# A new order table for the first loop of a fused two-layer kernel, with the setup's loads, memory sets and semaphore priming put in other places

## The chip, the cores and the metric

The kernel runs on one core of one Trainium2 chip, as one launch. The metric is the device time of that launch in microseconds (us), as a median of several runs. Lower is better.

## The reference

Sixteen images of 224x224 are cut into 196 patches each and projected to 192 channels, and 128 text tokens are put behind them: 324 tokens of 192 channels for each of 16 batches. Four residual blocks follow, each behind a layer norm.

```python
h = tok(x, W); h = concatenate([h, txt], axis=1)
h = h + L0_attn(layernorm(h))    # softmax over tokens, circular convolution with V (done by DFT), projection
h = h + L0_ffn(layernorm(h))     # 192 -> 768, gelu, -> 192
h = h + L1_attn(layernorm(h))    # 12 heads of 16; keys and values also of 196 shared tokens; softmax
h = h + L1_ffn(layernorm(h))     # 4 experts take half of the tokens each by router probability (top_k);
                                 # MLP 768 and a second attention on what they took, combined by the gate
```

## The kernel before, in words

The program has two software-pipelined loops over the 16 batches. The first does everything up to the router probabilities and the attention with shared tokens; the second does the experts' layer. In the turn between them (two iterations) both loops' work is woven together by position in their tables. TensorE (PE), ScalarE (ACT), VectorE (DVE), GpSimd (POOL) and SyncE (SP, which only issues DMAs) each run the same list of words, `ORDER_1` for the first loop, and each engine does in list order what it has to do for a word. The order among engines is set by semaphores alone.

`ORDER_1` has 15 slots. The words:

- `s`: one of 60 score products of a batch (PE, one matmul into one of two `sps` banks, L1356), then an exponential on ACT (L944). The third `s` waits for the exponential of the first.
- `a`: four attention sums of the four scores of the slot before (PE, L1371, eight half passes). Where a group of heads ends, ACT copies them to `av`.
- `m`: a product of queries and keys for the row maxima (PE, L1390, into one of three `mps` banks), reduced by DVE (L1214). Slots 0 to 4 do the heads of group 1, slots 5 to 9 those of group 2, slots 10 to 14 those of group 0 of the next batch. After the 18th of a group DVE does five small steps (L1220 to L1228); `r` transposes the result on PE, and ACT copies and stores it into `qpack` by a DMA. The scores of that group need it.
- `p`: one step of the expert choice on DVE, in six late iterations only.
- the rest are steps of the layers, each for the batch that `OFF_1` gives (this one, the one before, or one or two ahead): `tok`, `ln1`, `t1`, `zv`, `val`, `zs`, `zt`, `dft`, `of`, `inv`, `proj` make the first block two batches ahead; `ln2`, `t2`, `hid`, `out` the second, `ln3`, `t3`, `qk`, `todram`, `pack0`, `pack1` the queries and keys of the next batch, `v` and `pack2` those of this one; `den`, `recip`, `spread`, `norm`, `proj4`, `ln4`, `hx`, `t4`, `t5`, `log`, `exp`, `prob`, `prt` finish the batch before.

Steps write into two `lin` banks in turn, so each waits until the step two before it has been copied out.

The way from `qk` to the next maxima leaves the engines: ACT rounds a part to bf16 (`piece`, L854), DVE takes the rest (L1045), POOL splits that twice (L767, L769), SP stores the pieces (`scr_q` L596, `scr_k` L600) and, when they have landed, loads them as `qpack` and `kpack` for group 0 (L611, L614). Only then can the first `m` of slots 10 to 14 run.

The first iteration (number -2) does only the first block of batch 0, and number -1 adds the second and the queries of batch 0; full iterations are numbers 0 to 14.

Before the loop, SP primes 81 semaphores one after the other (L560, L561) and then issues all weight loads (L562 on): seven of them, `FIRST`, count on one semaphore, and PE waits for all seven before its first matmul, which is `tok`. DVE sets eight tensors to zero, and POOL loads the first batch and sets 13 tensors (L729 to L738), among them `kpack` twice, with `minus_half` last; `reciprocal_roots` (L771) needs `minus_half`.

Of the kernel before, what the change touches and what calls it, by code (L numbers as in the profile page):

```python
# [10 lines left out]
KC = 96  # L11
KP = 128
H, D = 12, 16
NK1 = N + SC
TK1, KT1 = P, 5
LAST1 = NK1 - (KT1 - 1) * TK1
# [17 lines left out]


ORDER_1 = (
# [15 lines left out]
)  # L52
OFF_1 = {"den": -1, "recip": -1, "spread": -1, "norm": -1, "proj4": -1, "ln4": -1, "hx": -1, "t4": -1, "t5": -1,
         "log": -1, "exp": -1, "prob": -1, "prt": -1, "v": 0, "pack2": 0, "hab": 0,
# [31 lines left out]
def number(name):  # L86

    tail = name[len(name.rstrip("0123456789")):]
    return int(tail) if tail else 0
# [172 lines left out]
def build(nc, A):  # L262
# [3 lines left out]
    with ctx:  # L266
# [3 lines left out]
        primed = []  # L270

        def signal(name, per=1, prime=1, first=0):
            s = Signal(ctx.enter_context(nc.semaphore(name)), per, prime - first, first)
            if per and prime:
                primed.append(s)
            return s


        w_tok = sb("w_tok", [128, 2, C])
        w_a = sb("w_a", [KP, 2, H])  # L280
        w_v0 = sb("w_v0", [KP, 2, C])
# [13 lines left out]
        ident = sb("ident", [128, 128])  # L295
        identb = sb("identb", [128, 128], bf16)
        dft = sb("dft", [KP, T, 2, 2, FW])
# [5 lines left out]
        bc = sb("bc", [128, GROUPS, N])  # L303
# [14 lines left out]
        xS = sb("xS", [KP, 2, NK1])  # L318
# [179 lines left out]
        def comes_first(att, j):  # L498

            return att is two and isinstance(j, int) and j == 0  # L500

        loads_first, loads, setup_dve, setup_pe, setup_act, setup_pool, sc_first, sc_rest, sc_mid, sc_pieces, sc_scr, sc_pack = (
            signal(n, 0) for n in ("loads_first", "loads", "setup_dve", "setup_pe", "setup_act", "setup_pool", "sc_first",
                                   "sc_rest", "sc_mid", "sc_pieces", "sc_scr", "sc_pack"))
        x_in = signal("x_in", 48, prime=0)
        hab_ready = signal("hab_ready", 16)
# [33 lines left out]
        MEMSETS_POOL, SETUP_POOL, SETUP_DVE = 13, 17, 9  # L540
        block = ctx.enter_context(nc.Block())

        FIRST = [(w_tok, A["w_tok"]), (ident, A["ident"]), (w_a, A["w_a"]), (w_v0, A["w_v0"]), (dft, A["dft"]),
                 (idft, A["idft"]), (w_p0, A["w_p0"])]
        LOADS = [
            (w_in, A["w_in"]), (b_in, A["b_in"]), (w_qkv, A["w_qkv"]), (w_out, A["w_out"]),
# [10 lines left out]

        @block.sync
        def _(sp):
            for s in primed:  # L560
                sp.sem_inc(s.sem, s.at(s.first, 0) + s.passed)  # L561
            for dst, src in FIRST:  # L562
                sp.dma_start(dst.ap(), src).then_inc(loads_first.sem, 16)
            for dst, src in LOADS[:4]:
# [158 lines left out]
        def _(pool):  # L723
# [3 lines left out]
                pool.dma_start(hin[:, 2, :], A["txt"][j, 2 * P - IMG:TXT, :]).then_inc(x_in.sem, 16)  # L727

            load_x(0)  # L729
            for n, (x, value) in enumerate(((of[64:KP, :, :, :], 0.0), (aT[KC:KP, :, :], 0.0), (aT[KC:KC + 1, :, :], 1.0),  # L730
                                            (xS[KC:KP, :, :], 0.0), (v1[:, :, :, :], 0.0),
                                            (kpack[KC:KP, :, :], 0.0), (yA[KC:KP, :, :], 0.0),
                                            (v1[:, 0:KT1 - 1, :, D:D + 1], 1.0), (v1[0:LAST1, KT1 - 1, :, D:D + 1], 1.0),
                                            (kpack[6 * D:6 * D + 3, :, :], 1.0), (yA[KC:KC + 1, :, :], 1.0),
                                            (bc[:, :, :], 1.0), (minus_half[:, :, :], -0.5))):
                if n:
                    pool.wait_ge(setup_pool.sem, n)
                nc.gpsimd.memset(x, value).then_inc(setup_pool.sem, 1)  # L738
            pool.wait_ge(setup_pool.sem, MEMSETS_POOL)

            def shared_pieces():

# [42 lines left out]
            def first_step(name, k, c, what, j, i):  # L785
                if name == "shared":
                    shared_pieces()
                    both_layers()
                elif name in ("ln1", "ln2", "ln3", "ln4"):
                    if k == 1:  # L790
                        reciprocal_roots(number(name) - 1, j)
                elif name == "xload":

                    front.filled(pool, i, "tok")
                    pool.wait_ge(ln1_done.sem, ln1_done.at(j - 1, 1))
                    front.emptied(pool, i, "proj_1")
                    pool.sem_inc(gate_pool.sem)
                    load_x(j)
                elif name == "hx":
                    pool.wait_ge(ln4_done.sem, ln4_done.at(j, 1))  # L800
                    pool.wait_ge(spilled.sem, spilled.at(j, 0))
                    nc.gpsimd.tensor_tensor(hx[:, :, :], ha[:, :, :], xna[:, :, :], ALU.add).then_inc(hx_ready.sem, 1)
                elif name == "qk":
                    parts(one, front, j, i, k)
# [18 lines left out]

        @block.scalar
        def _(act):
            def shared_keys():

                for m, p in enumerate(SCK):
                    act.wait_ge(setup_pe.sem, m + 1)
                    nc.scalar.copy(piece[0:p, m, 0, 0:SC], mps[0:p, m, 0:SC]).then_inc(sc_first.sem, 1)  # L830
                act.wait_ge(setup_pool.sem, MEMSETS_POOL)
                for m, p in enumerate((TK1, LAST1)):
                    act.wait_ge(setup_pe.sem, m + 3)
                    nc.scalar.copy(v1[0:p, KT1 - 2 + m, :, 0:D],
                                   sps[0:p, m, 0:C].rearrange("p (h d) -> p h d", d=D)).then_inc(setup_act.sem, 1)
# [141 lines left out]
        def _(dve):  # L977
# [5 lines left out]

            def shared_keys():

                dve.wait_ge(loads_first.sem, 16 * NFIRST)
                nc.vector.tensor_copy(identb[:, :], ident[:, :]).then_inc(setup_dve.sem, 1)
                for m, p in enumerate(SCK):
                    dve.wait_ge(sc_first.sem, m + 1)
                    nc.vector.tensor_tensor(rest[0:p, m, 0:SC], mps[0:p, m, 0:SC], piece[0:p, m, 0, 0:SC],  # L990
                                            ALU.subtract).then_inc(sc_rest.sem, 1)
# [287 lines left out]
        @block.tensor  # L1279
        def _(pe):  # L1280
            mm = nc.tensor.matmul
            pe.wait_ge(loads_first.sem, 16 * NFIRST)
            pe.wait_ge(setup_dve.sem, SETUP_DVE - 1)
            pe.wait_ge(setup_pool.sem, 3)

# [121 lines left out]
            def first_step(name, k, c, what, j, i):  # L1407
# [14 lines left out]
                elif name == "t1":  # L1422
                    pe.wait_ge(ln1_done.sem, ln1_done.at(j, 1))
                    transposes(front, i, what, k, xn1)
                elif name == "zv":
                    front.emptied(pe, i, "t1_1")
                    b = front.bank(pe, i, what)
                    for f in range(2):
# [200 lines left out]
```

## Time and profile before

| | us |
|---|---|
| median of 3 runs | 2089.15 (2087.38 to 2093.47) |
| the profiled execution, own time | 2096.61 |
| its span, first to last instruction | 2094.9 |
| PE busy | 1871.9 (89%) |
| DVE / ACT / POOL busy | 1247.5 / 1110.8 / 289.3 |

The span is what the trace covers; about 1.7 us of the execution's own time lie around it. The busy time of PE contains modelled ends of pipelined matmuls, so it overstates the work. In a view, a number in square brackets is the idle time of the engine just before the line's first instruction, and behind the arrow stands what ended it. Times of the trace count from the start of the span.

### The profile page before, as it was taken

The numbers are of one execution on the slowest core, as the hardware profiler recorded it, in microseconds if no ns is written. First come the engines' busy times: TensorE is split into PE (matmuls) and PEld (weight loads), VectorE is DVE, ScalarE is ACT, GpSimd is POOL, SyncE is SP. The second block draws the span as 40 slices with busy tenths as digits, with TensorE's granted clock in tenths as the row PEclk, the third lists the DMA queues.
The fourth block names the chain that finished last, engine by engine and source line by source line (L and its number), as shares of the span: only waits on it lengthen the run. The fifth ranks groups of instructions, "written<-read, shape, count | busy, mean of one in ns | idle before, by whom it ended". The sixth has DMA issues, their size and how long they took to land. (4 is left out here: it accounts for less than half of the span.)

```text
span 2094.9 us, 41506 instructions
## 1 busy us (share of the span) xinstructions
PE 1871.9 (89%) x11904; PEld 1260.5 (60%) x11904; DVE 1247.5 (60%) x3509; ACT 1110.8 (53%) x2583; POOL 289.3 (14%) x441
## 2 busy tenths in 40 slices
PE   3788998998998998998998997868999999999996
PEld 2565665675665675665675664435666666666664
DVE  2256566666566566666676674535767666666563
ACT  1244555555554555555555554445556565666663
POOL 4201111111111111111111110100100011001000
PEclk9799999999999999999999998879999999999998
DMA  4202212212212212212212202202433334333331
GB/s 151 68 16 58 69 32 71 64 32 74 61 32 67 64 36 69 67 34 69 65 36 69 68 27 76 75 17 80 103 100 90 87 93 119 82 101 101 100 86 36
DMA packets 161303, 143.61 MB, mean 69 GB/s; under 512 B 32284, under 2 KB 136488, under 8 KB 161064
## 3 DMA queue, kind: packets, MB, share of 16 engines
q1 hardware_dynamic: 157448, 136.69, 24.1%
q0 software_dynamic: 2304, 4.79, 1.0%
q8 instruction: 58, 0.95, 0.2%
q10 hardware_dynamic: 1440, 0.75, 0.1%
q14 instruction: 53, 0.43, 0.1%
HBM read 82.79 MB, written 50.16 MB: 63 GB/s over the span
## 5 line engine op out<-in xcount | busy, mean ns | idle before, releaser
L944 ACT ACTIVATE prob<-sps 108x324 f32<-108x324 f32 x1536 | 621.3, 439 | 506.6 <-PE sps L1356 470.3
L1214 DVE TENSOR_REDUCE mxh<-mps 108x1 f32<-108x324 f32 x1152 | 519.7, 489 | 319.2 <-PE mps L1390 315.4
L1356 PE MATMUL sps<-qpack,kpack 128*108 128x324 bf16 x1536 | 436.3, 318 | 33.5 <-ACT prob L944 25.6
L1390 PE MATMUL mps<-kpack,qpack 96*108 96x324 bf16 x1728 | 391.1, 296 | 46.7 <-DMA kpack<-scr_k 28.9
L1356 PEld LDWEIGHTS sps<-qpack,kpack 128*108 128x108 bf16 x1536 | 189.7, 127 | 228.2 <-ACT prob L944 163.0
L1371 PE MATMUL aps<-prob,v 128*32 128x324 f32 x3072 | 320.0, 460 | 2.4 <-DVE gmall L1202 1.1
L1390 PEld LDWEIGHTS mps<-kpack,qpack 96*108 96x108 bf16 x1728 | 215.8, 131 | 175.8 <-issue 57.6
L1342 PE MATMUL lin<-yT,w 128*128 128x324 f32 x576 | 184.0, 450 | 18.3 <-ACT g L844 14.1
L1214 DVE TENSOR_REDUCE mxs<-mps 108x2 f32<-108x392 f32 x288 | 160.0, 555 | 53.9 <-PE mps L1390 53.7
L1342 PEld LDWEIGHTS lin<-yT,w 128*128 128x128 f32 x576 | 102.4, 192 | 64.4 <-issue 33.2
L767 POOL CAST piece<-rest 128x324 bf16<-128x324 f32 x96 | 43.7, 456 | 700.2 <-DVE rest L1045 695.9
L1371 PEld LDWEIGHTS aps<-prob,v 128*32 128x32 f32 x3072 | 72.6, 109 | 104.5 <-issue 57.7
L1342 PE MATMUL lin<-xT,w_in 128*128 128x324 f32 x384 | 121.6, 449 | 0.5 <-ACT xT L840 0.5
L1332 PE MATMUL lin<-w,g 128*108 128x192 f32 x576 | 107.9, 328 | 0.7 <-PEq L136 0.7
L1332 PE MATMUL lin<-w_out,g 128*108 128x192 f32 x576 | 105.9, 327 | 1.6 <-PEq L136 1.6
L1332 PEld LDWEIGHTS lin<-w_out,g 128*108 128x108 f32 x576 | 92.3, 174 | 3.3 <-issue 2.1
L1332 PEld LDWEIGHTS lin<-w,g 128*108 128x108 f32 x576 | 91.2, 173 | 3.5 <-issue 1.1
L958 ACT COPY av<-aps 128x324 f32<-128x324 f32 x96 | 41.2, 429 | 98.0 <-PE aps L1371 73.0
L776 POOL TENSOR_SCALAR vars<-mean 108x3 f32<-108x3 f32 x64 | 15.5, 242 | 561.6 <-DVE mean L1012 560.9
L944 ACT ACT_TABLE_LOAD x64 | 82.1, 1283 | 14.9 <-PE sps L1356 13.1
L1315 PE MATMUL lin<-ident,xn 108*96 108x108 f32 x384 | 56.2, 263 | 36.9 <-DVE xn L1017 25.9
L1342 PEld LDWEIGHTS lin<-xT,w_in 128*128 128x128 f32 x384 | 69.8, 194 | 29.7 <-ACT g L844 6.4
(150 smaller groups left out, 2354.8 us busy)
## 6 DMA issues: line engine op xcount, KB each, us to landing
qpack<-scr_q SPq DMA_DIRECT2D x96, 243.0 KB, 3.2
kpack<-scr_k SPq DMA_DIRECT2D x96, 121.5 KB, 3.3
scr_q<-piece SPq DMA_DIRECT2D x32, 243.0 KB, 2.9
scr_k<-piece SPq DMA_DIRECT2D x32, 243.0 KB, 3.5
kpack<-scr_k SPq DMA_DIRECT2D x96, 81.0 KB, 3.1
bc<-rec_d SPq DMA_DIRECT2D x112, 60.8 KB, 2.4
scr_q<-piece SPq DMA_DIRECT2D x32, 162.0 KB, 3.3
scr_q<-piece SPq DMA_DIRECT2D x64, 81.0 KB, 3.0
```

The costliest lines, as they stand in the source:

```text
L767: nc.gpsimd.tensor_copy(piece[:, m, 1, :], rest[:, m, :]).then_inc(att.second.sem, 1)
L776: nc.gpsimd.tensor_scalar(vars4[:, n, 0], mean[n][:, :, 1], EPS4, None, ALU.add).then_inc(vars_known[n].sem, 1)
L944: nc.scalar.activation(prob[0:rows, n % NP, :], sps[0:rows, n % 2, 0:N], ACT.Exp, scale=SCALE).then_inc(att.exped.sem, 1)
L958: nc.scalar.copy(av[:, q, :], aps[:, 0:N]).then_inc(att.copied.sem, 1)
L1214: nc.vector.tensor_reduce(dst, src, AX.X, ALU.max, negate=True).then_inc(att.mps.free["dve"].sem, 1)
L1315: done = nc.tensor.transpose(b[0:KC, t * P:(t + 1) * P], src[:, t, k * KC:(k + 1) * KC], ident[0:P, 0:P])
L1332: done = mm(tiles2(b)[0:P, t % 2, :], acts[k][:, t * P:(t + 1) * P], weights[k], start=k == 0, stop=k == 5)
L1342: done = mm(b[0:size, 0:N], w[:, k, c:c + size], x[:, k, 0:N], start=k == 0, stop=k == 1)
L1356: mm(sps[0:rows, n % 2, 0:N], kpack[:, 4 * q + n % 4, k * att.rows:k * att.rows + rows], qpack[:, 4 * q + n % 4, :], start=True, stop=True ...
L1371: mm(aps[32 * hd:32 * hd + 32, 0:N], att.values[:, k, 4 * q + hd, :], prob[:, n % NP, :], start=k == 0, stop=k == kt - 1).then_inc(att.sum ...
L1390: done = mm(bank[0:P, s * SC:s * SC + k1 - k0], qpack[0:6 * D, 4 * q + hd, t * P:(t + 1) * P], kpack[0:6 * D, 4 * q + hd, k0:k1], start=Tr ...
```

## The change

The words of `ORDER_1` are the same, in another order and in other slots. In the setup, SP no longer primes the semaphores: ACT does it, at its own beginning. The seven first loads are split into two (`TOKENS`: `w_tok` and `ident`) and five (`FIRST`), on semaphores of their own; PE waits at the beginning for the two, and for the five at the first `zv`. POOL's memory sets are split: four (`of`, twice `aT`, `minus_half`) at once, and nine behind the reciprocal root of batch 0's first norm.

```diff
 ORDER_1 = (
-    "a ln2_1 m m m s v_0.0 s ln2_3 s s v_0.1 m s m p v_1.0 s recip s",
-    "t2_0 m a s t2_1 m m s",
-    "m s a s hid0 m hid1 pack2",
-    "m hid2 shared hid3 s m s hid4 m m p norm a m",
-    "hid5 m s s m proj4_0.0 m den proj4_0.1 s spread0 spread1 proj4_1 s s ln4_0 a s ln4_1 r ln4_2 hx s",
-    "out_0.0 m m out_0.1 a m p out_0.2 ln4_3 out_0.3 m out_1.0 m out_1.1",
-    "s m s ln3_0 tok.0 s tok.1 m m s hab t4_0 t4_1 ln3_1 s m a m log m s t5_0",
-    "exp p m s s ln3_3 t5_1 s m s a",
-    "s prob m t3_0 hc m s t3_1 a ln1_0 m qk0 m m qk1 s s qk2 s s ln1_1 p r",
-    "s todram s prt a s s",
-    "a s t1_0 t1_1 s s ln1_3 zv s",
-    "val_0.0 zs val_0.1 s val_1 pack0 zt s m m m dft_0.0 m p pack1 m a m s m dft_0.1 m s m dft_1.0 m m",
-    "m dft_1.1 s of s a s",
-    "s m s m m a s inv_0.0 s m p s m s m s",
-    "inv_0.1 inv_1.0 inv_1.1 s r proj_0.0 proj_0.1 proj_1 xload s ln2_0 a",
+    "den ln2_1 m m m spread0 a s s v_0.0",
+    "m s m s m p s v_0.1 s ln2_3 recip m m v_1.0 s s t2_0 a pack2 s",
+    "s a m s t2_1 s m m m s shared hid0 hid1",
+    "m m hid2 p hid3 hid4 hid5 norm m s m a s",
+    "m spread1 proj4_0.0 proj4_0.1 m proj4_1 s out_0.0 ln4_0 s out_0.1 out_0.2 ln4_1 s out_0.3 ln4_2 a s s r",
+    "m out_1.0 p m m m out_1.1 ln4_3 m a t4_0 ln3_0 t4_1 m s m s tok.0",
+    "ln3_1 m s tok.1 m m s t5_0 ln3_3 hab m s a",
+    "hc t5_1 log p s exp m m t3_0 t3_1 m prob hx s s m m qk0 m ln1_0 s qk1 s qk2 m s s a s ln1_1 todram s prt s s s p",
+    "r a s",
+    "a s s t1_0 t1_1 ln1_3",
+    "a",
+    "s zv s val_0.0 val_0.1 zs s val_1 m s m s zt m m m s dft_0.0 m p s m dft_0.1 m m s m dft_1.0 m m m s dft_1.1 m a",
+    "of pack0 s s a m s s m",
+    "m s a s inv_0.0 m p s",
+    "s pack1 inv_0.1 s inv_1.0 inv_1.1 r a s proj_0.0 xload proj_0.1 proj_1 ln2_0 s",
 )
...
-        FIRST = [(w_tok, A["w_tok"]), (ident, A["ident"]), (w_a, A["w_a"]), (w_v0, A["w_v0"]), (dft, A["dft"]),
+        TOKENS = [(w_tok, A["w_tok"]), (ident, A["ident"])]
+        FIRST = [(w_a, A["w_a"]), (w_v0, A["w_v0"]), (dft, A["dft"]),
                  (idft, A["idft"]), (w_p0, A["w_p0"])]
...
         def _(sp):
-            for s in primed:
-                sp.sem_inc(s.sem, s.at(s.first, 0) + s.passed)
+            for dst, src in TOKENS:
+                sp.dma_start(dst.ap(), src).then_inc(loads_tok.sem, 16)
             for dst, src in FIRST:
                 sp.dma_start(dst.ap(), src).then_inc(loads_first.sem, 16)
...
+            FEW = ((of[64:KP, :, :, :], 0.0), (aT[KC:KP, :, :], 0.0), (aT[KC:KC + 1, :, :], 1.0), (minus_half[:, :, :], -0.5))
+            REST = ((xS[KC:KP, :, :], 0.0), (v1[:, :, :, :], 0.0), (kpack[KC:KP, :, :], 0.0), (yA[KC:KP, :, :], 0.0),
+                    (v1[:, 0:KT1 - 1, :, D:D + 1], 1.0), (v1[0:LAST1, KT1 - 1, :, D:D + 1], 1.0),
+                    (kpack[6 * D:6 * D + 3, :, :], 1.0), (yA[KC:KC + 1, :, :], 1.0), (bc[:, :, :], 1.0))
...
+            memsets(FEW, 0)
...
                     if k == 1:
                         reciprocal_roots(number(name) - 1, j)
+                        if name == "ln1" and isinstance(i, int) and i == -2:
+                            pool.wait_ge(root_known[0].sem, root_known[0].at(j, 1))
+                            memsets(REST, len(FEW))
...
         def _(act):
+            for s in primed:
+                act.sem_inc(s.sem, s.at(s.first, 0) + s.passed)
...
-            pe.wait_ge(loads_first.sem, 16 * NFIRST)
+            pe.wait_ge(loads_tok.sem, 16 * len(TOKENS))
             pe.wait_ge(setup_dve.sem, SETUP_DVE - 1)
             pe.wait_ge(setup_pool.sem, 3)
...
                 elif name == "zv":
+                    if isinstance(i, int) and i == -2:
+                        pe.wait_ge(loads_first.sem, 16 * NFIRST)
```

## Rows read from the trace of the kernel before

**Rows 1.** The page, its first line.

```profile
span 2094.9 us, 41506 instructions
```

**Rows 2.** Windows: stretch, length, busy us of PE, PEld, DVE, ACT, POOL; clock; DMA; GB/s.

```profile
121.60:1276.00 1154.40, 1060.59 (x7093) 729.09 (x7091) 736.93 (x2148) 631.64 (x1512) 174.05 (x276) 0.99 0.20 55
1276.00:1416.00 140.00, 105.26 (x505) 56.84 (x506) 61.71 (x162) 55.98 (x124) 12.63 (x18) 0.76 0.21 54
```

**Rows 3.** Windows of one full iteration, cut behind `qk2` and at the first group-0 `m`.

```profile
434.90:480.70 45.80, 45.03 (x311) 32.26 (x304) 30.80 (x93) 27.87 (x64) 8.11 (x13) 1.00 0.16 49
480.70:494.40 13.70, 9.81 (x62) 5.25 (x60) 4.83 (x18) 7.90 (x22) 3.90 (x7) 1.00 0.52 144
494.40:513.00 18.60, 17.14 (x121) 12.34 (x125) 14.23 (x35) 7.01 (x19) 0.00 (x0) 1.00 0.04 9
```

**Rows 4.** Timeline of the start: start us, duration, engine, line, operation.

```profile
6.14 1.99 SPq L563 DMA_DIRECT2D w_tok<-in_w_tok  x1
...
6.54 0.33 DVE L981 MEMSET work<- 64x330 f32 x1
...
8.31 5.30 POOL L738 MEMSET kpack<- 32x6240 bf16 x1
...
10.54 0.43 SPq L563 DMA_DIRECT2D w_p<-in_w_p  x1
...
15.68 2.90 PE L1418 MATMUL lin<-w_tok,pT 128*108 128x192 f32 x8 [15.68 <-DMA w_p<-in_w_p]
...
20.79 0.31 DVE L1012 BATCH_NORM_AGGREGATE mean<-st 108x2 f32<-108x6 f32 x3 [0.73 <-DVEq L140]
...
21.79 0.11 POOL L738 MEMSET minus_half<- 108x6 f32 x1
22.21 0.25 POOL L776 TENSOR_SCALAR vars<-mean 108x3 f32<-108x3 f32 x1 [0.31 <-POOL minus_half L738]
```

**Rows 5.** DMA issues of the first 100 us, last column us from issue to landing.

```profile
w_tok<-in_w_tok SPq DMA_DIRECT2D x1, 192.0 KB, 4.0
w_p<-in_w_p SPq DMA_DIRECT2D x1, 192.0 KB, 5.1
```

**Rows 6.** Timeline of the way from `qk` to the next maxima, ACT, POOL, DVE, SP.

```profile
479.77 0.43 ACT L854 CAST piece<-lin 128x324 bf16<-128x324 f32 x1 [0.92 <-PE lin L1342]
...
480.26 0.80 POOL L769 TENSOR_TENSOR piece<-rest,piece 128x324 bf16<-128x324 f32 x1
...
480.38 0.71 DVE L1220 TENSOR_TENSOR mx<-mxh,mxs 108x12 f32<-108x12 f32 x1
...
481.09 4.94 SPq L596 DMA_DIRECT2D scr_q<-piece  x6
...
482.01 0.90 DVE L1045 TENSOR_TENSOR rest<-lin,piece 128x324 f32<-128x324 f32 x2
...
484.51 0.80 POOL L769 TENSOR_TENSOR piece<-rest,piece 128x324 bf16<-128x324 f32 x1
...
486.08 1.24 SPq L600 DMA_DIRECT2D scr_k<-piece  x2
```

**Rows 7.** Timeline of PE in the same iteration.

```profile
439.95 0.44 PE L1356 MATMUL sps<-qpack,kpack 128*108 128x324 bf16 x2
...
440.77 0.75 PE L1371 MATMUL aps<-prob,v 128*32 128x324 f32 x8
441.45 0.34 PE L1356 MATMUL sps<-qpack,kpack 128*108 128x324 bf16 x1
...
494.31 0.65 PE L1390 MATMUL mps<-kpack,qpack 96*108 96x324 bf16 x4 [1.16 <-DMA kpack<-scr_k]
```

**Rows 8.** Timeline of PE at `inv` and `proj`.

```profile
505.58 0.79 PE L1454 MATMUL lin<-idft,of 128*96 128x162 f32 x4 [0.55 <-DVE of L1132]
...
510.47 2.20 PE L1323 MATMUL lin<-w_p,aT 128*108 128x192 f32 x12 [0.74 <-DVE aT L1138]
```

**Rows 9.** Timeline of DVE at `recip`.

```profile
440.82 0.38 DVE L1054 RECIPROCAL drec<-dsm 108x36 f32<-108x36 f32 x1 [0.31 <-DMA dsm<-av]
```

More of the change, by code:

```diff
@@ L500, in comes_first @@
             return att is two and isinstance(j, int) and j == 0
-        loads_first, loads, setup_dve, setup_pe, setup_act, setup_pool, sc_first, sc_rest, sc_mid, sc_pieces, sc_scr, sc_pack = (
-            signal(n, 0) for n in ("loads_first", "loads", "setup_dve", "setup_pe", "setup_act", "setup_pool", "sc_first",
+        loads_tok, loads_first, loads, setup_dve, setup_pe, setup_act, setup_pool, sc_first, sc_rest, sc_mid, sc_pieces, sc_scr, sc_pack = (
+            signal(n, 0) for n in ("loads_tok", "loads_first", "loads", "setup_dve", "setup_pe", "setup_act", "setup_pool", "sc_first",
                                    "sc_rest", "sc_mid", "sc_pieces", "sc_scr", "sc_pack"))
@@ L729, in _, with memsets @@
             load_x(0)
[L730 to L739, printed above, removed]
+            FEW = ((of[64:KP, :, :, :], 0.0), (aT[KC:KP, :, :], 0.0), (aT[KC:KC + 1, :, :], 1.0), (minus_half[:, :, :], -0.5))
+            REST = ((xS[KC:KP, :, :], 0.0), (v1[:, :, :, :], 0.0), (kpack[KC:KP, :, :], 0.0), (yA[KC:KP, :, :], 0.0),
+                    (v1[:, 0:KT1 - 1, :, D:D + 1], 1.0), (v1[0:LAST1, KT1 - 1, :, D:D + 1], 1.0),
+                    (kpack[6 * D:6 * D + 3, :, :], 1.0), (yA[KC:KC + 1, :, :], 1.0), (bc[:, :, :], 1.0))
+            def memsets(sets, done):
+                for n, (x, value) in enumerate(sets):
+                    if n + done:
+                        pool.wait_ge(setup_pool.sem, n + done)
+                    nc.gpsimd.memset(x, value).then_inc(setup_pool.sem, 1)
+                pool.wait_ge(setup_pool.sem, done + len(sets))
+            memsets(FEW, 0)
+            assert len(FEW) + len(REST) == MEMSETS_POOL
             def shared_pieces():
@@ L984, in shared_keys @@
             def shared_keys():
-                dve.wait_ge(loads_first.sem, 16 * NFIRST)
+                dve.wait_ge(loads_tok.sem, 16 * len(TOKENS))
                 nc.vector.tensor_copy(identb[:, :], ident[:, :]).then_inc(setup_dve.sem, 1)
```

## The prediction, on record before the changed kernel ran

> **What bounds the kernel now.** I read the windows first. The eleven hundred microseconds of the first loop's full iterations have PE busy 1060.6 of 1154.4 us, DVE 736.9, ACT 631.6 [rows 2]: PE is the engine nearest to its limit. One full iteration, cut in three, lasts 45.8 + 13.7 + 18.6 = 78.1 us [rows 3], and 15 of them (numbers 0 to 14) carry the loop. The reader should see that the middle piece is different: PE is busy 9.8 of 13.7 us there, idle 3.9 us, while it is idle only 0.8 us in the 45.8 before it and 1.5 us in the 18.6 after it. The timeline of that piece shows why: the chain ACT `piece`, DVE `rest`, POOL's splits, SP's stores and loads [rows 6], at whose end PE's first group-0 `m` at 494.31 is released by the DMA of `kpack` [rows 7]. What PE has to do meanwhile is hidden; whatever shortens the chain, or fills it with work taken from elsewhere, shortens the iteration. The second such place is `inv` and `proj`, released by DVE's `of` and `aT` [rows 8]. The start has PE waiting until 15.68 for `w_p`, the last of seven loads [rows 4].
>
> **The start.** SP's first load is issued at 6.14, behind the priming [rows 4]. With the priming on ACT it can go at about 0.9, where the priming began (81 steps in 5.25 us). All loads move up by 5.2. `w_tok` landed 4.0 us after issue [rows 5], so it lands near 5, and `ident`, issued 2 us later, near the same time. PE still waits for DVE's eight sets, the last of which ends at 6.54 + 0.33 = 6.87 [rows 4]. ACT's priming ends near 6.1, before its first copy is due. So PE starts at 6.9 instead of 15.7: -8.7 us. The five other loads ended with `w_p` at 10.54 + 5.1 = 15.6 [rows 4, 5], now 10.4; `zv` wanted them 10.9 us after the first matmul, now at about 17, so that wait costs nothing. Second, the variance of the first norm was ready at 20.79 + 0.31 = 21.10, but POOL began its root at 22.21, behind `minus_half` [rows 4]. POOL is free now; elsewhere this step follows the variance by 0.2 us, so -0.9. The chain from the first `tok` to the end of iteration -2 is one of single steps with nothing beside it, so all of it goes through: -9.6 us in sum.
> The nine sets moved behind the root keep POOL for 16.2 us (from 5.53 to 21.73 before), so from about 13 to 30. What is queued behind them on POOL is `xload` of the next batch, which was due at 49.2 and is now due at 39.6: cover of 9 us. PE wants the sets at the end of iteration -2, later still. If that cover were gone, each us of it would cost one.
> A row bears on what else the sets may do. DVE's step L1220, which reads two tensors, took 0.71 us and ended at 481.09, beside a POOL instruction that ran from 480.26 to 481.06 [rows 6]; four sister steps behind it take 0.17 each. One engine held the other up. In iteration -2, DVE now works beside memory sets of up to 5.30 us [rows 4], which no row shows. If one such set held up DVE's norm or its `zexp` scaling, the cost would be 0 to 5.3 us. I take 0, for DVE's sets ran at 0.33 us beside POOL's before, and keep 5.3 for the range.
> The Trainium skill, page "SBUF — State Buffer", section "Who interferes with whom", says that DVE and GpSimd share one pair of SBUF ports as an exclusive lock: a GpSimd instruction that only writes does not disturb a DVE instruction with two SBUF inputs, but does block one in a two-port mode. By the first half the sets cost nothing, by the second a copy or scaling of DVE could wait a whole set, the 5.3 us above; the row at L1220 agrees with the lock.
>
> **The middle piece.** Before, the 18th `m` of group 2 stands before `qk1` in the table, so DVE does the closing steps (L1220 on) before it takes the `rest` of `qk1`: that began at 482.01, though ACT's piece was ready at 479.77 + 0.43 = 480.20 [rows 6]. 1.8 us lost. POOL's three pairs then end at 485.31, SP's stores at 487.32. In the new table the 18th `m` stands behind `qk2`, and `ln1_0` (0.87 us) stands between `qk0` and `qk1`. Step by step, counted from the end of `qk0`: DVE had the `rest` of `qk1` at +4.1; now it has its piece at +2.1, behind a reduction and `ln1_0` at about +3.0. POOL's second pair ends near +4.85 instead of +6.15. There SP takes over as the limit: six stores took 4.94 us and two more 1.24 [rows 6], and the first three are not earlier than before. I take 1.0 us gained, 0 and 1.8 as the bounds.
> Second, work moved into the piece. Before: 12 `s`, 2 `a`, `r`, `prt`, two `t1`, `zv`, three `val`, `zt` between `qk2` and the first group-0 `m`. Now: 13 `s`, 4 `a`, one `m`, and no `zt`. Before `qk2`, one `m` and a few `s` go the other way. An `s` takes 0.14 us of PE (the second in 0.44 less 0.30), an `a` 441.45 - 440.77 = 0.68 [rows 7]. So +0.14 + 2 x 0.68 + 0.15 - 0.25 = +1.4, and with `m` and `s` around `qk1` (one `m` less) about +1.2 net from the end of `qk0`. It fits: PE's idle time there was 3.9. Sum for the piece: -2.2 us an iteration. The `r` of group 2 is now further back, but `s` of group 1's end and two `a` follow it, 3.0 us of work before the first `s` of group 2 needs the DMA of `mT`; before it was 2.2 us of work. No new cost.
>
> **`of` to `proj`.** `dft_1.1` to `inv_0.0` had 2.7 us of PE work between; now 3.6. From the start of `inv_0.0` to `proj_0.0` passed 510.47 - 505.58 = 4.9 us [rows 8] with 3.7 of work; DVE was working off six `m` and the closing steps before it reached `aT`. Now four `m` stand behind `of`, and an `a` and an `s` stand between `inv_1.1` and `proj_0.0`: 3.9 of work, ready after about 4.2. That is -0.5 and -1.0: -1.5 us.
>
> **What crowds.** I counted, from the two tables, the places where PE meets an `m` with less than 1.65 us of its work since the one three before (three reductions of DVE of about 0.5): four before, nine now, short by 0.8 and 2.3 us in sum. For `s` with less than 0.9 us since the one two before: seven before (2.0 us), five now (1.5). Net +1.0. `log` now has only 0.8 us of work between it and `t3_1`, which needs its bank, and `proj4_0` to `out_0.0` 1.2 instead of 2.6: +0.3. Together +1.3 us, bounds 0 and 2.6.
> `den` and `spread0` now stand before `pack2` in SP's queue, so `pack2` waits for `recip`, some 7 us later than before; the `m` of group 2 want it 24 us into the iteration, so this is covered. The `recip` stands two `m` later on DVE, which waited 0.31 us for `dsm` [rows 9]; `den` is issued behind three `m` more, 0.4 us later. Nothing is taken for it.
>
> **The sum.** An iteration: -2.2 - 1.5 + 1.3 = -2.4 us; 15 of them -36. The start -9.6. In the turn (140 us, PE busy 105 [rows 2]) both tables' words are interleaved by position, and there is no `qk` of the first loop in it: 0, with 5 either way. The second loop's table is unchanged: 0. Together -46 us. The profiled execution has a span of 2094.9 [rows 1] in 2096.6, 7.5 above the median; I take the difference against the median: 2089 - 46 = 2043 us.
>
> **Rivals.**
> Only the start pays: the new table takes with its crowding what it gives (-3.7 + 3.7). For it speaks that the limit in an order of this kind moves quickly from one short place to the next, against it that the chain through DMA is seen as one long idle stretch. 2089 - 9.6 = 2079, with 2070 to 2082 for an iteration within 0.6 us.
> The crowding costs nothing: -3.7 x 15 - 9.6 = -65, 2024. For it: DVE is busy only 64% of the loop.
> The first sets hold up DVE at the start: up to 5.3 back, 2048. Its place is within the forecast's range; chance 0.1 of its own, by the page's second half. So far the trace bears out only the lock between two readers.
> Slower: `recip` at its new place stops DVE in front of the `m`. PE can run three `m` ahead and then stands, so each us that `dsm` comes later than DVE's turn costs one. Before, it came 0.31 us late [rows 9]. It decides from (36 + 9.6) / 15 = 3.0 us late in each iteration, and over 0.3% slower from 3.5: 2089 + 7 = 2096 and more. Against it: 0.4 to 0.9 us is what I count.
> The edit of the start doing nothing (PE held by the sets of DVE alone, which end at 6.87) can be excluded down to 8 us by the rows; I leave it in the ranges.
>
> **How the numbers follow.** Forecast, 2030 to 2060: 0.5. Between it and the start alone, 2060 to 2070: 0.1. Only the start: 0.17. No crowding, under 2030: 0.1. Slower by a stop that I have misjudged, `recip` the named one: 0.1, and 0.03 for no change. The change must exceed 0.3% (6 us), about what a measurement of this kernel can tell from none. Faster 0.86, same 0.04, slower 0.10. Range 2022 to 2080, which leaves out the slower cases and a little at the lower end.
>
> **What would show it.** PE's first matmul at 6.9 and POOL's first root 0.2 us behind the variance. The nine sets beside DVE's steps of iteration -2 with unchanged durations. A period near 75.7 us in place of 78.1; `rest` of `qk1` within 1 us of its piece; PE's idle time before the first group-0 `m` down to 2.5 us or less; the idle before `proj` gone. Wrong would be: DVE idle before `recip` for more than 1 us, more idle time of PE at `m` behind `mxh` in slots 1 to 3 and 5, or a turn longer than 145 us.

## The result, and the profile after

The changed kernel takes 2019.8 us (median of 4 runs, 2012.9 to 2025.5), the kernel before beside it 2091.3 (4 runs, 2087.4 to 2096.6): a ratio of 0.9655, 95% interval 0.9617 to 0.9693, so 71.5 us less. Forecast were 46 us less, 2043, with a range of 2022 to 2080. The sign was right; the size was not, and the time lies just below the range. One of the four runs of `n_max_crowded` below took 6039 us and is left out of its numbers; no other run of any kernel stood apart like this.

The page of the changed kernel, its first part (the profiled execution took 2019.94 us):

```profile
span 2018.3 us, 41467 instructions
...
PE 1844.5 (91%) x11904; PEld 1249.0 (62%) x11904; DVE 1257.5 (62%) x3509; ACT 1080.0 (54%) x2555; POOL 288.9 (14%) x441
```

The two profiled spans differ by 76.6 us [rows 1], 5 more than the medians, since the profiled execution of the kernel before was a long one. To see where, I took an instruction that occurs once for each batch, ACT's exponential `zexp` (in the first block of batches 0 to 15). Its row of the changed kernel, with the first and the last start, and then that of the kernel before:

```profile
L912 ACT ACTIVATE zexp<-lin,nmz x16: 521/521/522, 28.1 to 1134.4; 12x324 f32<-12x324 f32 x16
```

```profile
L900 ACT ACTIVATE zexp<-lin,nmz x16: 522/522/522, 29.5 to 1199.4; 12x324 f32<-12x324 f32 x16
```

With the starts between them, the first `gelu` of the second loop's batch 1 as the end of the turn, and the start of DVE's last step as the end of the last stretch (3.8 us before the end of the span in both), the time splits like this. The last two columns are the time at the lower clock, 1.2 GHz, inside each stretch (us):

| stretch | before | after | less | forecast | at 1.2 GHz before | after |
|---|---|---|---|---|---|---|
| start, to `zexp` of batch 0 | 29.5 | 28.1 | 1.4 | 9.6 | 0 | 12.9 |
| to batch 1 | 69.0 | 64.3 | 4.7 | 0 | 27.4 | 16.5 |
| to batch 2 | 77.6 | 67.9 | 9.7 | 2.4 | 13.6 | 4.8 |
| to batch 15, 13 periods | 1023.3 | 974.3 | 49.1 | 31.2 | 13.7 | 34.1 |
| rest of the loop and the turn | 167.4 | 159.8 | 7.6 | 2.4 | 41.0 | 30.7 |
| to the end | 724.2 | 720.2 | 4.0 | 0 | 47.8 | 41.0 |

The last line is no effect of the change: its stretch came out between 719.6 and 728.0 us in the kernels below that have the new table, and between 719.5 and 724.2 in those that have the old one. The reader should see two errors of opposite sign: the start gave 8 us less than forecast, the loop much more.

One full iteration of the changed kernel, cut as in [rows 3], the next iteration whole, and the stretches that answer to [rows 2]:

```profile
408.25:451.20 42.95, 42.25 (x282) 30.90 (x281) 30.43 (x92) 24.09 (x58) 7.84 (x13) 1.00 0.19 52
451.20:464.30 13.10, 11.22 (x79) 5.66 (x78) 5.89 (x19) 8.29 (x23) 4.17 (x7) 1.00 0.54 152
464.30:481.92 17.62, 17.44 (x130) 12.58 (x129) 13.75 (x35) 8.33 (x21) 0.00 (x0) 1.00 0.04 8
481.92:558.97 77.05, 73.74 (x490) 51.38 (x488) 50.08 (x145) 40.82 (x101) 12.00 (x19) 0.96 0.20 57
1200.00:1342.00 142.00, 103.45 (x555) 55.26 (x552) 62.66 (x170) 64.89 (x144) 12.05 (x19) 0.83 0.23 60
115.00:1210.00 1095.00, 1046.34 (x7081) 723.71 (x7081) 739.34 (x2141) 596.90 (x1477) 173.12 (x275) 0.98 0.21 59
```

At full clock an iteration is 42.95 + 13.10 + 17.62 = 73.7 us, not 75.7 as forecast and 78.1 before. PE is idle 0.7, 1.9 and 0.2 us in the three pieces (0.8, 3.9 and 1.5 before). The second iteration has the same instructions and takes 3.4 us more; its clock is 0.96, and a cut in steps of 10 us shows why (two rows of it):

```profile
510.00:520.00 10.00, 9.62 (x82) 7.40 (x80) 9.12 (x27) 4.96 (x13) 2.49 (x3) 1.00 0.14 49
520.00:530.00 10.00, 9.40 (x44) 5.84 (x44) 7.87 (x26) 5.99 (x17) 3.70 (x6) 0.83 0.27 84
```

The clock drops to 1.2 GHz for part of 520 to 530, and again in 540 to 550, while PE was busy 9.62 of the 10 us before the first of them and 8.04 of the 10 before the second. Such stretches add up to 34 us between 150 and 1130 us, 14 before. That is why the mean of the 13 periods is 74.9 and not 73.7.

PE's waits between 300 and 1100 us (what it waited for: us in sum, times, longest), first before, then after:

```profile
PE mps L1390 <- DMA kpack<-scr_k: 15.1, 10, 1.9
PE sps L1356 <- ACT prob L944: 12.5, 30, 0.6
PE lin L1315 <- DVE xn L1017: 10.9, 10, 1.1
PE lin L1323 <- DVE aT L1138: 6.9, 10, 0.7
PE lin L1454 <- DVE of L1132: 5.3, 10, 0.6
```

```profile
PE mps L1402 <- DMA kpack<-scr_k: 14.7, 11, 2.6
PE lin L1327 <- DVE lg L1187: 5.1, 10, 0.6
PE sps L1368 <- ACT prob L956: 3.5, 18, 0.2
PE mps L1412 <- DVE mp L1240: 2.7, 7, 0.4
PE mps L1402 <- DVE mxh L1226: 1.0, 6, 0.2
```

Here lies the largest surprise: the wait at the end of the chain through DMA, on which I had built the forecast, is hardly smaller. Those for `of` and `aT`, nearly all of that for the norm's `xn`, and most of that of the scores for ACT's exponentials are gone. A new one, `lg`, stands behind `log` (I had priced its bank, together with that of `out_0.0`, with 0.3 us of crowding): 0.5 us an iteration.

The start of the changed kernel, to be read beside [rows 4]:

```profile
0.88 0.42 SPq L562 DMA_DIRECT2D w_tok<-in_w_tok  x1
...
6.54 0.33 DVE L993 MEMSET work<- 64x330 f32 x1
...
8.46 2.86 PE L1430 MATMUL lin<-w_tok,pT 128*108 128x192 f32 x8 [8.46 <-DMA hin<-in_txt]
...
13.20 0.31 DVE L1024 BATCH_NORM_AGGREGATE mean<-st 108x2 f32<-108x6 f32 x3 [0.40 <-DVEq L140]
...
13.79 0.25 POOL L782 TENSOR_SCALAR vars<-mean 108x3 f32<-108x3 f32 x1 [8.16 <-DVE mean L1024]
14.12 0.90 POOL L788 TENSOR_TENSOR root<-vars,minus_half 108x3 f32<-108x3 f32 x1
15.05 8.21 DVE L1029 TENSOR_SCALAR xn<-hin,mean,root 108x192 f32<-108x192 f32 x3 [1.54 <-POOL root L788]
15.07 0.96 POOL L741 MEMSET xS<- 32x1040 f32 x1
16.09 1.70 POOL L741 MEMSET v<- 128x1920 f32 x1
17.85 5.29 POOL L741 MEMSET kpack<- 32x6240 bf16 x1
...
24.31 5.29 POOL L741 MEMSET kpack<- 3x6240 bf16 x1
...
28.89 0.89 DVE L1122 TENSOR_SCALAR zexp<-zexp,zrec 12x324 f32<-12x324 f32 x1
```

POOL's root follows the variance (13.20 + 0.31) by 0.28 us, as forecast. PE begins at 8.46, not 6.9: it waits for the first batch, which POOL loads. And DVE's three scalings `xn`, begun at 15.05, end at 23.26, 0.12 us behind the set of `kpack` that ended at 23.14. Taken singly they last 1.10, 1.83 and 5.43 us, beside sets of 0.96, 1.70 and 5.29, and each ends 0.11 to 0.12 us behind its own set. The third:

```profile
17.82 5.43 DVE L1029 TENSOR_SCALAR xn<-hin,mean,root 108x192 f32<-108x192 f32 x1
```

Likewise the scaling of `zexp` ends at 29.78, behind the next set of `kpack` (29.60). The kernel with the old setup does the first in 0.96 and the second in 0.38 us (next section).

### The profile page after: what moved, and what is told of

It is laid out like the page before. It is cut to its first block and busy times, and to the rows that moved or that the text cites. A ratio compares the mean times of both kernels' runs of the same rounds, so it can differ in the third digit from the quotient of the medians.

```text
span 2018.3 us, 41467 instructions
## 1 busy us (share of the span) xinstructions
PE 1844.5 (91%) x11904; PEld 1249.0 (62%) x11904; DVE 1257.5 (62%) x3509; ACT 1080.0 (54%) x2555; POOL 288.9 (14%) x441
## 5 line engine op out<-in xcount | busy, mean ns | idle before, releaser
L1402 PE MATMUL mps<-kpack,qpack 96*108 96x324 bf16 x1728 | 385.2, 297 | 47.2 <-DMA kpack<-scr_k 24.6
L1368 PEld LDWEIGHTS sps<-qpack,kpack 128*108 128x108 bf16 x1536 | 184.8, 127 | 213.3 <-ACT prob L956 118.0
L1383 PE MATMUL aps<-prob,v 128*32 128x324 f32 x3072 | 298.9, 454 | 3.9 <-DVEq L140 1.1
L1354 PE MATMUL lin<-yT,w 128*128 128x324 f32 x576 | 183.7, 450 | 13.5 <-ACT g L856 11.5
L1383 PEld LDWEIGHTS aps<-prob,v 128*32 128x32 f32 x3072 | 66.4, 108 | 85.9 <-issue 62.5
L1354 PE MATMUL lin<-xT,w_in 128*128 128x324 f32 x384 | 111.8, 441 | 0.2 <-ACT g L856 0.2
L1460 PE MATMUL lin<-vz,dft 128*82 128x204 f32 x384 | 83.3, 358 | 0.7 <-DVEq L140 0.7
```

Source lines behind the costliest of these rows:

```text
L1354: done = mm(b[0:size, 0:N], w[:, k, c:c + size], x[:, k, 0:N], start=k == 0, stop=k == 1)
L1368: mm(sps[0:rows, n % 2, 0:N], kpack[:, 4 * q + n % 4, k * att.rows:k * att.rows + rows], qpack[:, 4 * q + n % 4, :], start=True, stop=True ...
L1383: mm(aps[32 * hd:32 * hd + 32, 0:N], att.values[:, k, 4 * q + hd, :], prob[:, n % NP, :], start=k == 0, stop=k == kt - 1).then_inc(att.sum ...
L1402: done = mm(bank[0:P, s * SC:s * SC + k1 - k0], qpack[0:6 * D, 4 * q + hd, t * P:(t + 1) * P], kpack[0:6 * D, 4 * q + hd, k0:k1], start=Tr ...
L1460: done = mm(b[0:FW, 256 * c:256 * c + C + H], dft[:, t, k, c, :], vz[:, t, :], start=t == 0, stop=t == T - 1)
```

## The experiments

Ratios are to the kernel before, timed in the same session, with 95% intervals. "Iteration" is the undisturbed one, at full clock, the median of a trace, from `zexp` to `zexp`. The changed kernel has three such iterations among its 13 (73.2 to 73.6 us). The four traces of kernels that share its table have medians of 73.6 to 74.0 (`table_only` 73.8, `sets_after_zs` 73.9, `sets_first` 74.0), so a difference to 73.6 that is given below may be up to 0.4 us too large.

### The parts alone: setup_only and table_only

`setup_only` has the old table with the new setup, `table_only` the new table with the old setup.

> The new setup with the old order table. Theory: in the changed kernel POOL's nine memory sets hold up DVE's first norm (8.2 us for three steps that took 0.96), so the new setup brings little: the first exponential of zexp 1.4 us earlier, 0 to 3 us in all, 2088 to 2091. Rival: the setup also shortens the following iterations (priming, loads out of the way), 5 to 15 us.

> The new order table with the old setup. Theory: the table carries nearly all of the gain, -68 to -72 us, 2020 to 2023. Rival: the two parts need each other, and the table alone gives 50 to 60 us.

Measured: 2090.0 us, 0.9995 (0.9976 to 1.0014), and 2023.0 us, 0.9680 (0.9648 to 0.9712). In `setup_only` `zexp` of batch 0 starts at 28.65, 0.9 us earlier than before. The whole gain lies in the table, the two together add up within their error, and my 9.6 us for the start are not there. From `setup_only` and from `table_only`, the same step of DVE:

```profile
15.64 8.21 DVE L1029 TENSOR_SCALAR xn<-hin,mean,root 108x192 f32<-108x192 f32 x3 [1.53 <-POOL root L788]
```

```profile
23.47 0.96 DVE L1017 TENSOR_SCALAR xn<-hin,mean,root 108x192 f32<-108x192 f32 x3 [3.41 <-POOL root L782]
```

The table also shortens the turn by itself (158.9 us of the stretch that had 167.4), and so it does the second interval (69.4 for 77.6).

### Where the sets stand: sets_after_zs and sets_first

```diff
 # sets_after_zs: POOL's nine sets behind zexp's scaling of batch 0
-    pool.wait_ge(root_known[0].sem, root_known[0].at(j, 1))
+    pool.wait_ge(zs_ready.sem, zs_ready.at(j, 1))
     memsets(REST, len(FEW))
 # sets_first: all nine directly behind the four
     memsets(FEW, 0)
+    memsets(REST, len(FEW))
 # and behind the root
-    pool.wait_ge(root_known[0].sem, root_known[0].at(j, 1))
-    memsets(REST, len(FEW))
```

> The changed kernel with the nine memory sets behind the scaling of zexp of batch 0 instead of behind the first root. Theory (a set of POOL blocks DVE's tensor_scalar steps): the first norm takes 0.96 us again, zexp scaling 0.38, and everything behind it is 7 to 8 us earlier, 2012. Theory's further sign: of, whose steps read two tensors, now lies beside the sets and keeps 0.55 us a step, since the sets read nothing. Rival (any DVE step with a tensor in SBUF is blocked): of takes up to 5 us longer and the gain is 2 to 3 us.

> The changed kernel with all 13 memory sets at the beginning, minus_half fourth. Theory: POOL's root waits for the sets until about 21.8, as before the change, the norm follows undisturbed at 23.1, zexp about where it is in the changed kernel plus 1 us: 0 to +2 us, 2021. Rival: the sets cost DVE's own memory sets and the token copy more than that, +5 us.

Measured: 2015.9 us, 0.9651 (0.9615 to 0.9688), and 2024.1 us, 0.9668 (0.9630 to 0.9705). From `sets_after_zs`:

```profile
14.61 0.96 DVE L1029 TENSOR_SCALAR xn<-hin,mean,root 108x192 f32<-108x192 f32 x3 [1.53 <-POOL root L788]
20.75 0.52 ACT L912 ACTIVATE zexp<-lin,nmz 12x324 f32<-12x324 f32 x1 [2.91 <-DVE nmz L1117]
21.59 0.38 DVE L1122 TENSOR_SCALAR zexp<-zexp,zrec 12x324 f32<-12x324 f32 x1
22.02 0.96 POOL L741 MEMSET xS<- 32x1040 f32 x1 [7.45 <-DVE zexp L1122]
24.80 5.29 POOL L741 MEMSET kpack<- 32x6240 bf16 x1
29.18 0.55 DVE L1133 TENSOR_TENSOR ta<-vf 82x384 f32<-82x384 f32 x1
```

`zexp` starts at 20.75 instead of 28.06: with no set beside them the scalings take 0.96 and 0.38 us again, and the 7.3 us come back. `ta`, a step of DVE with two inputs, takes 0.55 us though the set of `kpack` runs from 24.80 to 30.09. So the cause is the set beside a scaling, not a set beside any step of DVE. The Trainium skill, page "SBUF — State Buffer", section "Who interferes with whom", says just this: a GpSimd instruction that only writes holds up no two-input step of DVE but blocks one in a two-port mode for its whole length; the trace agrees, with 8.21 for 0.96 us on one side and 0.55 us unchanged on the other, but no row says in which mode a scaling ran. Nor do the rows show the scaling as the later of the two: each of the three begins 0.02 us before its set (15.05 and 15.07, 16.07 and 16.09, 17.82 and 17.85), and it is the scaling that waits. In `sets_first` the norm stands behind all sets, undisturbed, and begins at 23.53, where it began before the change. In the medians these 7 us are small: 2015.9 against 2019.8, with intervals that overlap; the place of the sets is shown by the trace, its worth in the time only roughly.

### The middle piece: n_max_before_qk1, n_sums_out, n_norm_behind_qk2

All three edit slot 7 of the new table: the 18th `m` of group 2 back before `qk1`; one `a` moved out, before `qk0`; the norm behind `qk2`.

```diff
-m m qk0 m   ln1_0 s qk1 s qk2 m s s a s
+m m qk0 m m ln1_0 s qk1 s qk2   s s a s          (n_max_before_qk1)
+m m a qk0 m ln1_0 s qk1 s qk2 m s s s            (n_sums_out)
+m m qk0 m s qk1 s qk2 ln1_0 m s s a s            (n_norm_behind_qk2)
```

> The changed kernel with one word of slot 7 moved back: the 18th m of group 2 before qk1 and not behind qk2, as in the old table. Theory (the chain of DMAs sets the first group-0 m, and DVE's closing steps in front of the rest of qk1 lengthen it): the time from the end of qk0 to that m goes from 15.8 to 16.5 us or more, an iteration becomes 0.7 to 1.0 us longer, 10 to 15 us in all, 2031 to 2035. Rival (SP's stores are the limit, DVE's place has no part in it): under 0.2 us an iteration, within 3 us.

> The changed kernel with one a (0.68 us of PE) moved from behind qk2 to before qk0, out of the stretch that the DMAs set. Theory (PE waits there for the DMA whatever it does meanwhile): +0.7 us an iteration, +10 us, 2030. Rival (that stretch is set by PE and ACT, not by the DMA): no change within 3 us.

> The changed kernel with ln1_0 behind qk2 and not between qk0 and qk1. Theory (DVE's place in the chain sets the loads): the rest of qk1 begins at +2.6 us from the last pass of qk0, not +3.4; POOL is free from +3.5, so the pieces end 0.6 us earlier; -0.3 to -0.6 us an iteration, -5 to -9 us. Rival (SP's stores, which take 3.3 us behind the first three, or t1's norm, now later, become the limit): within 3 us, or slower.

Measured: `n_max_before_qk1` 2050.9 us, 0.9821 (0.9788 to 0.9854), an iteration 2.0 us longer on average, twice what I had expected. All of it lies between the start of `qk0` and the first group-0 `m`: 18.8 us (median) in place of 16.7. Counted from the third of the four passes of `qk0` (here and below), DVE begins the `rest` of `qk1` at 5.5 us instead of 3.4, POOL ends at 8.8 instead of 6.7, and SP issues the loads at 13.5 instead of 11.5. The 18th `m` at its old place thus costs 2 us in the new table; in the old one I had read 1.8 us lost in [rows 6] and taken 1.0 of them.

`n_sums_out` 2032.6 us, 0.9724 (0.9693 to 0.9756): the time between `qk0` and the `m` stays at 16.7 us with one `a` less in it, and the kernel as a whole loses 12.8 us. Its iteration takes 75.1 us, 1.1 to 1.5 more, for an `a` of 0.68 us that is no longer hidden and 0.4 us more of idle time between `proj` and `qk0`, where it now stands. In the traces the 13 periods account for 5.9 us only, since it had 10 us at 1.2 GHz there and the changed kernel 34; another 6.0 lie in the turn, where it is the other way about (44 and 31). Work put into this piece is free up to the chain's length.

`n_norm_behind_qk2` 2013.1 us, 0.9647 (0.9612 to 0.9683), cannot be told from the changed kernel. POOL ends 0.65 us earlier (6.01 for 6.66), but SP issues the loads at 11.44, as before 11.46: SP's own stores are the limit there, as the prediction had it.

### The same move in the old table: o_max_behind_qk2

```diff
-ln1_0 m qk0 m m qk1 s s qk2   s s ln1_1 p r
+ln1_0 m qk0 m   qk1 s s qk2 m s s ln1_1 p r
```

> The kernel before with one word of slot 8 moved: the 18th m of group 2 behind qk2 and not before qk1. Theory (this word is a large part of the table's gain; taking it back in the changed kernel cost 2 us an iteration): the rest of qk1 about 1 us earlier, POOL's pieces and SP's loads with it, -1.0 to -1.5 us an iteration, -15 to -22 us, 2070. Rival (it pays only in the new table, where ln1_0 stands before qk1 too): within 5 us of before.

Measured: 2083.3 us, 0.9962 (0.9947 to 0.9976), 8 us less, where 15 to 22 were expected and under 5 by the rival. The chain did get shorter (loads issued 11.3 us behind `qk0`, not 12.4), and PE's waits between 300 and 1100 us show one thing that became of it:

```profile
PE mps L1400 <- DVE mp L1228: 19.9, 7, 2.8
PE sps L1356 <- ACT prob L944: 12.7, 30, 0.6
PE mps L1400 <- issue: 8.1, 4, 2.7
PE lin L1323 <- DVE aT L1138: 6.9, 10, 0.7
```

No wait for `kpack` is left, but PE now stands up to 2.8 us at `r`, whose maxima DVE has not yet closed. The new table puts `r` into the next slot, with seven `s`, an `a` and `prt` between the 18th `m` and it, and there it waits 0.4 us at most (the row L1412 of the changed kernel). No kernel moved `r` with the `m` in the old table, so what that is worth alone is not shown.

The other thing is the clock. Two iterations of `o_max_behind_qk2`, from `qk0` to `qk0`:

```profile
477.90:556.40 78.50, 72.47 (x489) 50.24 (x489) 49.90 (x144) 42.86 (x103) 11.99 (x19) 0.98 0.20 55
948.50:1025.60 77.10, 71.57 (x488) 49.74 (x488) 52.26 (x156) 42.92 (x103) 12.02 (x19) 1.00 0.20 57
```

The second, the only one of the twelve between 240 and 1180 us with no time at 1.2 GHz, takes 77.1 us, 1.0 less than the undisturbed iteration of the kernel before, in spite of the stand at `r`: that is the gain that was expected. In the eleven others the clock is at 1.2 GHz for 3.4 us or more. In nine of them this begins 9.2 to 9.4 us behind the start of `qk0`, 2 us after PE's stand at `r` and inside the very piece that the chain had set, and these nine take 78.1 to 78.6 us. It is not this execution alone: all ten executions have a mean granted clock of 0.957 to 0.965, all fifteen of the kernel before in that session 0.967 to 0.973. Whether it is the stand at `r` that brings the lower clock about, no run shows.

### `of` to `proj`: o_sum_before_proj

In the old table the `a` at the end of slot 14 goes before `proj_0.0`.

```diff
-inv_0.1 inv_1.0 inv_1.1 s r   proj_0.0 proj_0.1 proj_1 xload s ln2_0 a
+inv_0.1 inv_1.0 inv_1.1 s r a proj_0.0 proj_0.1 proj_1 xload s ln2_0
```

> The kernel before with only the a of slot 14 moved from the end to before proj_0.0, as the new table has it. Theory (PE waits there 1.2 us for aT and the a fills it): -0.7 us an iteration, -10 us, 2079. Rival (the a only changes places with a wait of its own, or delays proj and the norm behind it): within 3 us.

Measured: 2090.9 us, 1.0006 (0.9987 to 1.0025). The wait for `aT` is gone (6.9 us among PE's waits above, now none), the idle time from `inv_0.0` to `proj_0.0` falls by 0.6 to 0.7 us, and that between `proj_1` and `t2_0` grows by as much: the `a` had covered the next norm. The rival was right: a single `a` only changes which wait it covers.

### What crowds: n_max_crowded and old_first_five_slots

```diff
 # n_max_crowded, slot 5 of the new table
-m out_1.0 p m m m out_1.1 ln4_3 m a
+m m m m m out_1.0 p out_1.1 ln4_3 a
```

`old_first_five_slots` has the new setup and the new table, but slots 0 to 4 are the old ones without `hx`, and slot 5 begins `out_0.0 m out_0.1 m out_0.2 m out_0.3 m out_1.0 p out_1.1`.

> The changed kernel with five m in a row in slot 5 instead of 1 + 3 + 1 around out_1. By the counting rule of the prediction (1.65 us from each m to the third behind it) this costs about 2 us an iteration, +25 to +30 us, 2047. Theory now: the rule overstates, since DVE has its slack back by the next m; the stall is as large, but much of it is taken from waits that follow (bank waits of s and out), so +0.5 to +1 us an iteration, +8 to +15.

> The changed kernel with slots 0 to 4 of the old table (without hx), the four out_0 steps laid between the m of slot 5, and slots 6 to 14 new. Theory (the gain comes from the stretch of the DMAs and from of to proj, both in the new slots): the undisturbed period stays within 0.5 us of the changed kernel's 73.6, within 8 us in all. Rival (the first five slots carry a third of the gain, since fewer s follow each other there): +1.2 us an iteration, +18.

Measured: `n_max_crowded` 2032.5 us, 0.9726 (0.9688 to 0.9764), 13 us more than the changed kernel. An iteration takes 74.4 us, 0.4 to 0.8 more, where my counting rule says 2. The stretch from `hid0` to `out_1.1` has 0.7 us more idle time, and part of that comes back right behind it.

`old_first_five_slots` 2041.3 us, 0.9778 (0.9739 to 0.9816), 21 us more than the changed kernel, as the rival had it: an iteration takes 74.8 us, 0.8 to 1.2 more, and the interval from `zexp` of batch 1 to that of batch 2 is 74.4 instead of 67.9 (with 15.6 us of it at 1.2 GHz instead of 4.8). PE's waits between 300 and 1100 us:

```profile
PE mps L1402 <- DMA kpack<-scr_k: 14.7, 11, 1.7
PE sps L1368 <- ACT prob L956: 8.3, 30, 0.4
PE lin L1327 <- DVE lg L1187: 5.5, 11, 0.6
```

The scores wait 8.3 us for ACT, against 3.5 with the new slots. So the first slots, which I had put down as more crowded, are the less crowded ones.

### A version that takes both up: loads_behind_x

The new table with the norm behind `qk2`, the sets behind `zexp`, and SP's five other loads held back until the first batch has landed:

```diff
+            sp.wait_ge(x_in.sem, 48)
             for dst, src in FIRST:
```

> What the runs point to, together: the changed kernel with the nine memory sets behind the scaling of zexp, with SP's five first loads behind the landing of the first batch's x and text, and with ln1_0 behind qk2. Theory: the token product starts at about 6.9 us and not at 8.0 to 8.7, zexp at 19.5 and not at 28.1, and the table as in the run with ln1_0 moved: 2003 to 2010. Rival: loads that begin 4 us later hold up zv, or the norm's new place costs; then 2015 or more.

Measured: 2004.4 us (5 runs, 2000.9 to 2005.7), 0.9587 (0.9562 to 0.9611), the best of all. SP's first load behind that wait is issued at 5.23, so the batch has landed by then, and PE starts when DVE's sets end:

```profile
5.23 0.33 SPq L565 DMA_DIRECT2D w_a<-in_w_a  x1
...
6.98 2.54 PE L1431 MATMUL lin<-w_tok,pT 128*108 128x192 f32 x7 [6.98 <-DVE work L994]
```

`zexp` of batch 0 is at 19.8, 9.7 us before the old kernel's. That is the 9.6 us forecast for the start: both things in the way were named by the runs, and with both removed the step holds. It also shows that the first batch, which landed at 8.3 us in the changed kernel, was held up by SP's five other loads, issued there from 1.82 on: with them PE's first matmul began between 7.96 and 8.76 us in nine traces of the new setup, without them at 6.98.

## Why the prediction was right and wrong

**The start** (-9.6 forecast, -1.4 measured) failed at one term: "I take 0" for the sets beside DVE's scalings. It measured 7.25 us at the norm (8.21 - 0.96), and 0.5 at the scaling of `zexp` (0.89 - 0.38), which lies behind the start that the table counts to. The argument was that DVE's own sets ran at 0.33 us beside POOL's; a set that reads nothing says little about a scaling. The rival had the right mechanism with a chance of 0.1, and too small a bound: 5.3 for one set, where three scalings each waited for one of three sets in a row. A smaller miss, 1.5 us: PE's start at 6.9 assumed that the first batch had landed, which the old kernel's loads, begun at 6.14, had never tested.

**The middle piece** (-2.2 an iteration) held. Worked out from the starts of PE's matmuls (median over the iterations, less the least time that the same work took in either kernel), the idle time from `qk0` to the first group-0 `m` fell by 1.8 us, 2.1 in the iterations at full clock. The chain is 0.9 us shorter (forecast 1.0), and 1.3 us of work are more in it (1.2). Each half cost time when it was undone, and more than its term: 2.0 us an iteration for the `m`, 1.1 to 1.5 for one `a` of 0.68. What was not said: PE's wait for `kpack` stays, and the move of the `m` makes PE stand at `r` unless `r` stands further back; in the old table it gave 8 us of the expected 15 to 22, with more time at 1.2 GHz beside it.

**`of` to `proj`** (-1.5): the idle time in these two stretches fell by 1.7 us. The size is right, but the reason that I gave is not enough: an `a` put there by itself gave nothing, as its wait moved on to the next norm. That the new table keeps the gain must lie in what it has behind that place; which word does it was not tested.

**What crowds** (+1.3, bounds 0 and 2.6) is the step that made the time wrong. The idle time of all other stretches changed by -0.2 us an iteration, and by about -0.6 in the iterations at full clock, below the lower bound. A table-side count of too-close `m` and `s` takes each as a stall of its own; `n_max_crowded` shows one such stall at 0.4 to 0.8 us for a counted 2, some of it given back behind it, and `old_first_five_slots` shows that the first slots are worth -0.8 to -1.2 us an iteration, the opposite of what the count gave. Over the 13 periods the 1.5 us between the two are 19.5, the largest single part of the excess. The bounds were bounds of the rule, and not of what could happen: nothing excluded a gain.

**The first intervals and the turn** (0 and -2.4 taken, 4.7, 9.7 and 7.6 measured). I took the forecast iteration for all alike. The interval with the first full one gained four times as much; with the old first five slots 6.5 of its 9.7 us are lost again. But a part of these gains is clock: the two intervals and the turn had 27.4, 13.6 and 41.0 us at 1.2 GHz before and 16.5, 4.8 and 30.7 after. In the traces with the new table the interval to batch 2 takes 66.9 us with 1.5 of them at 1.2 GHz (`sets_after_zs`) and 69.4 with 8.3 (`table_only`), 0.37 us for each us; by that estimate 3 of the 9.7 us are clock, and 4 of the 6.5 that `old_first_five_slots` lost. For the turn, `setup_only`, with the old table and the changed kernel's 30.7 us at 1.2 GHz, takes 166.3 us, so there 6.6 of the 7.6 remain; but `n_sums_out`, with the new table, takes 165.7 with 44.4. Which words of the table shorten these stretches, and what in them moves the clock, was not tested and stays open.

**Clock.** In the 13 periods part of the gain was taken back: the ten with a stretch at 1.2 GHz take 74.3 to 76.4 us, the three without 73.2 to 73.6, and the new loop has 34 us at that level instead of 14. How much of that is the change is open: the profiled executions of the other kernels with nearly the same table had 7, 14, 14, 24 and 27 us, so much of it differs from run to run. Over the whole span the two traces have the same mean granted clock, 0.965.

**The signs** named ahead: root behind the variance, `rest` of `qk1` (within 1 us of its piece), idle time before the `m` (1.9 us, forecast 2.5 or less) and before `proj` (gone) came as said; the first matmul at 6.9, unchanged steps beside the sets, and a period of 75.7 did not. Of the slower rival nothing was seen: no stop at `recip`, and the turn is 142 us long, not over 145.

The sum, in the terms of the forecast: 46 less, +8.2 for the start, -17.9 for the 13 periods, -4.7 and -7.3 for the two first intervals, -5.2 for the last part of the loop with the turn, -4.0 of scatter behind it, gives 76.9, against the 76.6 between the spans.

## What to carry to other kernels

When big memory sets of POOL are moved off the path, look at what DVE does beside them: here each scaling of one tensor by per-partition scalars stood until the set beside it was through, three scalings through three sets, while steps with two inputs passed. When work is reordered in a table that several engines share, a stall that is covered in one place is often one that its cover had been hiding in another; judge a move with its neighbours, and let the range include a gain for all that one can only count. Compare the granted clock of both kernels before a wait is called the reason that a move paid little. A load that is begun earlier can compete with the one that the first instruction really needs.

## What the runs showed of the hardware

- Three scalings of 108x192 values, 0.38 us each alone and 0.96 in a row, took 8.21 us beside three memory sets of POOL (0.96, 1.70 and 5.29 us) that followed each other with 0.06 us between them: 1.10, 1.83 and 5.43 us, one scaling to a set, each ending 0.11 to 0.12 us behind its set. DVE's reduction over 324 elements (0.48 us, as elsewhere) inside the second `kpack` set, and its two-input steps (0.55 us), were not slowed.
- An iteration with 0.96 of mean granted clock took 77.05 us, its neighbour at 1.00 took 73.67.
- With one `m` moved, the mean granted clock of a kernel fell from 0.967 to 0.973 (15 executions) to 0.957 to 0.965 (10); in its trace a stretch of 3.4 us at 1.2 GHz lay at the same place in most iterations.
- SP's first load took 1.99 us to issue at 6.14 [rows 4], and 0.42 at 0.88.
- The first batch's three loads landed at 8.3 us when SP's five weight loads ran beside them, and by 5.23 when these waited.
